# Last cross attention: where VectorE adds the output projection into the residual and takes its statistics

## What is computed

```python
x = x + L0_xattn(layernorm(x), ctx)     # 16 heads of 16
x = x + L0_ffn(layernorm(x), ...)       # self attention, then 8 experts of which 2 per row
x = x + L1_xattn(layernorm(x), ctx)     # 8 heads of 64, no q/k/v bias, scale 1/8
x = x + L1_ffn(layernorm(x))            # rounding to an FP6 grid in blocks of 32, then one 256x256 product and a bias
```

```python
q, k, v = norm(x) @ Wq, ctx @ Wk, ctx @ Wv
x = x + softmax(q k^T / 8) v @ Wo + bo
y = norm(x); y = round_to_grid(y / s) * s     # s: one scale per 32 values
out = x + y @ weight.T + bias
```

## Time and profile before

| | |
|---|---|
| median of 3 runs | 2145.3 us (2142.04 to 2145.58) |
| the profiled execution | 2148.31 us, of which the span of the instructions is 2146.3 us |
| busy share of the span | PE 93%, DVE 65%, ACT 48%, POOL 41% |
| last cross attention | from about 1387 us to the end; its loop of 28 steps from about 1470 to 2090 us |
| granted TensorE clock, mean | 0.971 of full speed |

### The profile page before, as it was taken

One profiled execution on the slowest core, in us unless ns is written; L12 is line 12 of the kernel. 1 busy time (PEld: TensorE's weight loads), 2 busy tenths in 40 slices (PEclk: granted clock), 3 DMA queues, 4 the chain that ended last, 5 costly groups with the idle time before them and its releaser, 6 DMA issues. The chain is left out here.

```text
span 2146.3 us, 61038 instructions
## 1 busy us (share of the span) xinstructions
PE 1999.6 (93%) x21235; PEld 1659.7 (77%) x21236; DVE 1390.0 (65%) x3586; ACT 1022.8 (48%) x2370; POOL 889.4 (41%) x1479
## 2 busy tenths in 40 slices
PE   5999999996899999589999999779999999999996
PEld 4888888885677777479999999657777777777774
DVE  5777777773688888543333333247887878788875
ACT  2555555553444444223223232246666666666662
POOL 4454554541466666400000000145656666665651
PEclk9999999998999999799999999979999999999998
DMA  7223323251400000111111111210111111011100
GB/s 209 90 85 103 95 92 105 82 210 29 143 22 21 21 21 21 51 57 37 34 39 34 37 37 34 87 34 22 37 31 36 31 29 39 27 39 29 36 20 9
DMA packets 98810, 118.87 MB, mean 55 GB/s; under 512 B 9794, under 2 KB 91458, under 8 KB 98626
## 3 DMA queue, kind: packets, MB, share of 16 engines
q1 hardware_dynamic: 92610, 103.43, 15.8%
q0 software_dynamic: 6144, 14.69, 2.3%
HBM read 67.36 MB, written 50.72 MB: 55 GB/s over the span
## 5 line engine op out<-in xcount | busy, mean ns | idle before, releaser
L1245 ACT ACTIVATE e_act_T<-ps_quad,fc_b 128x128 f32<-128x128 f32 x504 | 136.8, 383 | 313.3 <-PE ps_quad L1310 313.3
L1310 PEld LDWEIGHTS ps_quad<-e_xT,e_w_now 128*128 128x128 f32 x2016 | 236.4, 193 | 7.9 <-DVE e_xT L1279 4.1
L1310 PE MATMUL ps_quad<-e_xT,e_w_now 128*128 128x128 f32 x2016 | 237.4, 276 | 3.5 <-DVE e_xT L1279 3.5
L1325 PE MATMUL ps_out<-w,e_act_T 128*128 x1008 | 228.1, 379 | 0.8 <-DVE e_y L1287 0.8
L1423 POOL COPY c_index<-slot 112x1 uint32 (+1 forms) x64 | 19.4, 332 | 477.7 <-POOLq L1208 477.7
L419 ACT ACTIVATE a_probsT<-ps_quad 125x1792 f32<-125x1792 f32 x96 | 159.9, 1665 | 100.6 <-PE ps_quad L579 100.6
L1276 DVE COPY e_w_now<-w 128x2048 f32 x63 | 77.3, 1227 | 200.2 <-PE ps_quad L1310 190.3
L1325 PEld LDWEIGHTS ps_out<-w,e_act_T 128*128 128x128 f32 x1008 | 186.6, 190 | 24.0 <-issue 1.2
L1450 POOL TENSOR_TENSOR c_kL<-c_kT,c_kH 128x376 fp32r<-128x376 f32 x128 | 126.3, 986 | 172.0 <-ACT c_kH L1502 171.4
L206 ACT ACTIVATE c_probs<-ps_quad,c_negmax 112x375 f32<-112x375 f32 x256 | 144.0, 571 | 29.7 <-DVE c_negmax L167 29.7
L1497 ACT ACTIVATE c_kT<-ps_proj 128x376 f32<-128x376 f32 x128 | 61.9, 484 | 182.8 <-PE ps_proj L258 181.4
(11 more groups left out here) (308 smaller groups left out, 5331.6 us busy)
## 6 DMA issues: line engine op xcount, KB each, us to landing
slots<-a_zeros SPq DMA_DIRECT2D x60, 512.0 KB, 4.9
a_cT<-in_ctx_t SPq DMA_DIRECT2D x32, 375.0 KB, 3.6
c_cT<-in_ctx_t SPq DMA_DIRECT2D x32, 375.0 KB, 3.2
w<-in_fc_t SPq DMA_DIRECT2D x2, 4096.0 KB, 20.1
w<-in_fc_t SPq DMA_DIRECT2D x8, 1024.0 KB, 11.7
e_xg<-slots SPq DMA_DIRECT2D x63, 128.0 KB, 2.0
slots<-e_y SPq DMA_DIRECT2D x63, 128.0 KB, 1.7
out<-c_fo SPq DMA_DIRECT2D x32, 112.0 KB, 1.9
```

The source lines that it names most:

```text
L1245: last = act.activation(act_T[par][:, c * TILE:(c + 1) * TILE], hidden[par][:, c // 4, (c % 4) * TILE:(c % 4 + 1) * TILE], ACT.Gelu, bias= ...
L1310: last = pe.matmul(hidden[par][:, c // 4, (c % 4) * TILE:(c % 4 + 1) * TILE], w1_now[:, k, c * 128:(c + 1) * 128], xT[par][:, k, :], start ...
L1325: last = pe.matmul(y_ps[:, 0:D], act_T[1 - par][:, c * TILE:(c + 1) * TILE], w2[:, bass.ds(e, 1), c, :].rearrange("p a d -> p (a d)"), sta ...
```

## The change

VectorE's addition of `o` into the residual and the statistics of the sum are moved from the end of step b-1 (after `f`) into unit 0 of step b, behind the maxima of (b, 0) and ahead of the scaling of (b-1, 3). The batch on which they work is the same, so its number is b-2 as seen from step b. Nothing is added or removed on VectorE, and no other engine's program changes.

```diff
                     for u in range(U):
                         if exists(b):
                             core.dve_max(dve, b, u)
+                        if u == 0 and exists(b - 2):
+                            x = row(residual, b - 2)
+                            dve.wait_ge(o_biased, b - 1)
+                            dve.tensor_tensor(x, x, o[:, :], ALU.add).then_inc(x_ready, 1)
+                            dve.wait_ge(x_ready, b - 1)
+                            norm_f.dve_moments(dve, b - 2, x)
                         at = core.behind(b, u, 1)
                         if exists(at[0]):
                             core.dve_normalise(dve, *at)
...
                             dve.tensor_tensor(f[:, :], proj[0:T, D:2 * D], bf[0:T, :], ALU.add).then_inc(f_biased, 1)
-                        if u == 3 and exists(b - 1):
-                            x = row(residual, b - 1)
-                            dve.wait_ge(o_biased, b)
-                            dve.tensor_tensor(x, x, o[:, :], ALU.add).then_inc(x_ready, 1)
-                            dve.wait_ge(x_ready, b)
-                            norm_f.dve_moments(dve, b - 1, x)
```

## The result

The changed kernel took 2131.47 us in the median of 4 runs (2127.27 to 2135.63), against 2144.97 us for the kernel before (4 runs, 2142.04 to 2145.58): a ratio of 0.9940, 95% interval 0.9917 to 0.9962. That is 13.5 us less; 12.0 us less, 2133.3 us, was forecast, and the range was 2130.5 to 2141.0. Two more sets of runs gave 0.9937 (0.9925 to 0.9949) and 0.9934 (0.9919 to 0.9949).

A forecast was written before the change was run, and what follows sets the result against it. TensorE, idle 11.6 us mostly waiting for ScalarE's value copy, was taken to bound the last cross attention loop. 13 x 0.64 + 15 x 0.25 = 12.0 us off 2145.3 gave 2133.3 us, range 2130.5 to 2141.0.

The forecast's parts named there:

- Which wait bounds the stage, and what removes it: Last cross attention loop: TensorE idles 11.5 us in 28 waits for ScalarE's value copy; earlier maxima of unit 0 remove them.
- the distance: Start of the value chunk's last product to next key projection: 1.73 us (even), 1.34 (odd), to become 1.09 in all steps.
- the list of waits: Profile list for the last stage's loop, 28 waits, 11.5 us; ScalarE's value copy should vanish or leave only tenths.
- The sum: TensorE's gain over the last stage: 13 even steps at 0.64 us plus 15 others at 0.25, 12.0 us.
- The pause at the loop's jump: VectorE pauses 0.40 us at the loop's jump back in even steps; it would now lie ahead of unit 0's maxima.
- The addition: VectorE's moved residual addition in even steps: about 0.7 us instead of 1.23, ending at 1813.05.
- The cover at line 1684: TensorE's line 1684 waits for VectorE's xd: margin 0.60 us, forecast 0.30 after a gain of 0.64 and xq 0.34 earlier.
- GpSimd's delayed root: Square root delays the low key tile of unit 2 by 0.7 to 1.3 us, covered by ScalarE's late input.
- The addition and line 1445: Of the addition's 1.23 us, 0.82 is waiting for GpSimd's line 1445; maxima reading PSUM do not contend with it.
- The first rival: The addition's 1.23 us belong to the instruction, not GpSimd; even gain 0.30, total 7.7 us, 2137.6 us; chance 0.19.
- the second rival: Collisions of VectorE with GpSimd's low key tiles make xq 0.5 to 0.7 us late; within 4 us of 2145; chance 0.11.
- the third: VectorE's path through GpSimd's root to xd becomes the longer one; xq 0.76 us late, 11 us slower, 2156; chance 0.08.

The follow-up runs named there:

- the last kernel: Changed kernel with GpSimd's two indirect transfers of a step moved ahead of the low key tile of unit 2; ratio to before 1.0001.
- the last two kernels: Changed kernel with GpSimd's line 1445 behind its square root, ratio 1.0095; changed kernel with the indirect transfers ahead of unit 2's low key tile, 1.0001.
- statistics alone: Kernel before with only the statistics moved behind the maxima of unit 0, the addition left ahead of them; ratio 0.9929, stage 659.16 us.
- one instruction more ahead: Kernel before with one extra VectorE maximum over the bias tile ahead of the maxima of unit 0; ratio 1.0033, stage 678.71 us.

## Why the prediction was right

*Which wait bounds the stage, and what removes it.* Right in each step. The wait was all of TensorE's idle time, the maxima's end moved ahead of the key copy, the distance fell to 1.08 or 1.09 in all steps, and the list of waits lost its line.

*The sum.* 12.0 us forecast for the stage, 14.05 measured. The distances alone give 0.64 and 0.25 us per step, as forecast, and 12.0 us over the stage. The rest is the delay of unit 2: the kernel before had its key copies 0.07 to 0.19 us behind the product and the changed kernel's first execution had them at 0.04, and the change did not cause that, since the second execution of the same changed kernel had them 0.13 to 0.27 behind and a stage of 659.04, 10.1 us under before. The forecast lies between the two. So 12.0 of the 14.05 us are the forecast's mechanism, and the other 2 are a matter of which executions are compared.

*The pause at the loop's jump.* Wrong in its place. It was carried along at 0.40 us ahead of the maxima, but they start 0.33 us after f in even steps too. In odd steps the prediction's sum has a slip: it starts the maxima at 1833.64, where f's 0.34 is counted twice; by its own rows it is 1833.30, 0.67 us after o, and that is what was measured. Neither mattered, as the maxima were done before the key copy ends in any case. The pause shows where the short statistics stand ahead of the jump, and doesn't where f or the addition does. That an instruction of 0.4 us or more hides the jump is my reading; the runs show only where the pause is and isn't.

*The addition.* The mechanism was right and the size in even steps wrong. Taken at about 0.7 us, with an end at 1813.05, it took 0.41: without the pause it is issued 0.05 us ahead of line 1479 and not behind it. With it the statistics, the root and xq came earlier than forecast: xq starts 3.62 us after o, where it was 4.62, and the margin at line 1684 is 0.50 to 0.56 where 0.30 was forecast. None of this reached TensorE.

*The cover at line 1684.* It held, but the check looked at one of two waits. The same line also waits for ScalarE's xT, which in the even step of before is

```profile
1825.45 0.36 ACT L1526 ACTIVATE c_xT<-ps_turned 128x224 f32<-128x224 f32 x1
```

It ends at 1825.81. With the 0.10 us that the last kernel shows behind it, the margin was 0.32 us there and not the 0.60 us of xd, less than the gain of 0.64. It cost nothing because xT came earlier by as much: it ends 14.69 us after o where it was 15.39, as ScalarE's value copy ahead of it in unit 2 waits for TensorE (0.41 us before, 0.42 in the changed kernel). The margin is 0.31 us still. The prediction did not ask this; on this wait it was right without a reason given.

*GpSimd's delayed root.* Its cover held: the low key tile of unit 2 still starts when ScalarE's high part is there, 6.14 us after o (1801.95), after a wait of 1.71 us.

*The addition and line 1445.* Shown: 1.23 us beside line 1445, 0.42 with it moved, 0.41 behind the maxima, all with addresses computed in the loop. The first rival, that the 1.23 us belong to the instruction, is out. The maxima, which read PSUM, take 0.93 us beside line 1445 and 0.94 without it. The rule that the Trainium skill gives for this ("SBUF — State Buffer", section "Who interferes with whom") agrees with these rows. The same section lets `tensor_scalar` contend only in its two-port modes; lines 178 and 245, which have one SBUF tensor as input beside one or two numbers per row, were held up too (2.98 and 1.75 us), and no run shows in which mode they ran.

*The second and third rivals.* Neither came to pass, but the last two kernels show that both are real, and the unchanged lines around the change decide it. With the transfers earlier, VectorE collides with GpSimd's low key tiles and the gain is gone (ratio 1.0001, stage 668.37): that is the second rival, the one called "nothing measurable". With line 1445 later the kernel is slower than before, as in the third (1.0095), but by another path: xq is 2.04 us late, and yet the maxima of unit 1 were late first. What was wrong in the third is the price: it let each delay of xq run through to xd. Three more instructions behind the statistics made xq 0.72 us later and xd not at all, because line 178 was waiting for GpSimd anyway. In no kernel's loop does TensorE wait for xd alone, so the one-to-one price that both rivals use beyond the margin is not shown.

*Left open.* What the delay of unit 2 is. It falls on GpSimd's second indirect transfer; it was there in four profiled executions (before, changed the second time, statistics alone, one instruction more ahead) and not in four others with the transfer at the same 0.05 us behind line 1167's start. The four with the transfer elsewhere didn't have it. The chips put some order into this. The changed kernel the second time, statistics alone and one instruction more ahead ran on one chip and all have the delay; the changed kernel the third time and the two with one and three instructions behind the statistics ran on another chip, and none has it. On the first of these chips the kernel with line 1445 later, whose transfer is elsewhere, was free of it, and its timed median was 5.3 us under the changed kernel's; on the second their medians were within 0.6 us of each other. So every run on these two chips fits one reading: the delay comes only where the transfer stands at that place of the step, and only on the first of the two chips. That is three executions against three, each chip in runs of its own, and for the first runs of before and of the changed kernel no chip is on record; it is not shown, and nothing says what in a chip would do it.

## What to carry to other kernels

Follow the one wait of the bounding engine back to where it starts, and ask how late each step of that path may be: here 0.64 us too late was all there was to win, and three different edits (the whole move, half of it, or GpSimd's line 1445 out of the way of an addition) each won it. Two edits that each win it are not to be added up: put together they lost 32 us against either alone, because GpSimd's instruction then fell on another VectorE one. Check every wait of the instruction that has the margin: here a second one, for xT, was nearer than the one looked at. Extra work on an engine that would wait for another one anyway can be free, and a move on a third engine that no semaphore connects with it can cost a microsecond per step.

## What the runs showed of the hardware that I had not expected

- A VectorE pair of 0.74 us lasted 2.98 us beside a pair of GpSimd instructions of 1.94 us, and a single one of 0.40 us lasted 1.75 us beside one of 1.01 us. The VectorE one is not only slowed, it ends with GpSimd's, 0.22 and 0.16 us behind its recorded end. So these two engines meet at more than semaphores. The recorded starts don't tell who came first: the second scaling of the pair started 0.50 us ahead of line 1445 and line 245 0.58 us ahead of line 1450, more than the 0.41 and 0.40 us that they take otherwise, and both were held all the same.
- The addition, issued 0.11 us before line 1445's recorded end (1754.45), took 0.41 us and no longer. So VectorE can go on before the recorded end of a GpSimd instruction. The rows of before say the same: the addition that was held ended 0.28 us after line 1445, less than the 0.42 us that it takes otherwise, so it went on about 0.13 us ahead of that end (my estimate, from these three numbers). The forecast of 0.7 us for the moved addition had added 0.28 us behind line 1479 without this.
- The same kernel, in two executions, has VectorE and ScalarE start up to 1.0 and 0.2 us later at one place of each step, with the offsets ahead of it the same within 0.02 us; 4 us of 655.
